# A small matrix product moved off TensorE: partial products on ScalarE and VectorE, one sum over partitions left

## The reference

```python
q = xt @ Wq.T
scores = scale * einsum('bhqd,bhkd->bhqk', qh, qh)
logits = (scores * cmask + (1.0 - cmask) * NEG) * rmask
attn = softmax(logits, axis=-1)
ctx = einsum('bhqk,bhkd->bhqd', attn, qh)
out = ctx @ Wo.T          # then x + out
```

## Time and profile before

| | |
|---|---|
| time, median of 3 runs | 1602.4 us (1602.02 to 1602.5) |
| span of the profiled execution | 1599.3 us |
| PE busy | 1513.2 us (95%) |
| PEld busy | 1185.6 us (74%) |
| DVE busy | 1198.6 us (75%) |
| ACT busy | 877.7 us (55%) |
| POOL busy | 1336.3 us (84%) |
| mean granted TensorE clock | 0.981 of full speed |

### The profile page before, as it was taken

The page is one execution under the profiler, slowest core; times in us unless marked ns, Lnnn a source line. Parts: engine busy times, 40 slices in busy tenths (PEclk is TensorE's granted clock), DMA queues, the critical chain, the costliest instruction groups (busy, mean ns, idle before and its releaser), DMA issues. The chain is left out here.

```text
span 1599.3 us, 32587 instructions
## 1 busy us (share of the span) xinstructions
PE 1513.2 (95%) x10636; PEld 1185.6 (74%) x10636; DVE 1198.6 (75%) x2676; ACT 877.7 (55%) x2189; POOL 1336.3 (84%) x1078
## 2 busy tenths in 40 slices
PE   5789999999999999999999999999999999999985
PEld 4568777777777777777777777777777777777753
DVE  4487787878778787877878787787878778787753
ACT  4345556565655656565565656556565655656441
POOL 3377989898898989889898988989898898988875
PEclk9779999999999999999999999999999999999998
DMA  4423444544444454444445444444554444454411
GB/s 137 104 65 96 108 120 109 130 123 111 118 113 117 112 130 123 110 118 115 116 113 130 123 110 119 114 117 111 130 123 111 119 113 117 111 130 96 111 53 55
DMA packets 93809, 179.07 MB, mean 112 GB/s; under 512 B 24704, under 2 KB 24832, under 8 KB 93632
## 3 DMA queue, kind: packets, MB, share of 16 engines
q1 hardware_dynamic: 64448, 109.71, 29.2%
q0 software_dynamic: 29184, 67.17, 14.9%
HBM read 36.77 MB, written 33.55 MB: 44 GB/s over the span
## 5 line engine op out<-in xcount | busy, mean ns | idle before, releaser
L835 ACT ACTIVATE small_Pt<-scores,small_kbias 108x270 f32<-108x270 f32 x1280 | 550.9, 483 | 343.7 <-PE scores L1245 334.8
L985 DVE TENSOR_REDUCE small_mxp<-max_scores 108x1 f32<-108x270 f32 x1280 | 546.7, 435 | 250.7 <-PE max_scores L1226 228.9
L646 POOL TENSOR_TENSOR small_Pacc<-small_Pacc,small_Pt 108x540 f32<-108x540 f32 x384 | 520.8, 1356 | 122.3 <-ACT small_Pt L835 116.6
L1226 PE MATMUL max_scores<-small_ops 128*108 128x270 f32 x1280 | 420.1, 336 | 22.2 <-DVE small_mxp L985 21.6
L1257 PE MATMUL ctx_psum<-small_Pt,small_V 108*64 108x270 f32 x2560 | 317.5, 395 | 0.0
L1017 DVE RECIPROCAL small_rsum<-small_rsum 128x67 f32<-128x67 f32 (+1 forms) x512 | 240.8, 532 | 66.3 <-ACT small_rsum L771 66.3
L1242 PE MATMUL scores<-small_ops 128*108 128x270 f32 x1280 | 281.1, 294 | 8.7 <-ACT small_Pt L835 7.0
L1226 PEld LDWEIGHTS max_scores<-small_ops 128*108 128x108 f32 x1280 | 221.3, 175 | 89.9 <-issue 38.4
L1257 PEld LDWEIGHTS ctx_psum<-small_Pt,small_V 108*64 108x64 f32 x2560 | 187.4, 139 | 109.0 <-issue 4.6
L1245 PE MATMUL scores<-small_ops 128*108 128x270 f32 x1280 | 265.4, 289 | 0.0
L1242 PEld LDWEIGHTS scores<-small_ops 128*108 128x108 f32 x1280 | 193.5, 174 | 38.4 <-ACT small_Pt L835 20.1
(11 more groups left out here) (129 smaller groups left out, 2273.2 us busy)
## 6 DMA issues: line engine op xcount, KB each, us to landing
small_ops<-small_H SPq DMA_DIRECT2D x512, 135.0 KB, 2.5
small_ops<-small_L SPq DMA_DIRECT2D x256, 135.0 KB, 2.5
small_ops<-small_mrow SPq DMA_DIRECT2D x128, 2.1 KB
small_xg<-x_rows,small_idx POOLq DMA_INDIRECT x80, 3.9
small_xtail<-x_rows,small_idx POOLq DMA_INDIRECT x80, 5.0
out_rows<-small_xtail,small_idx POOLq DMA_INDIRECT x80, 3.7
out_rows<-small_xg,small_idx POOLq DMA_INDIRECT x80, 4.1
wqT_sb<-wqT SPq DMA_DIRECT2D x1, 1024.0 KB, 5.4
```

Source lines behind the costliest of these rows:

```text
L646: nc.gpsimd.tensor_tensor(acc, other, t["Pt"][:R, p0], ALU.add).then_inc(pacc_step, 1)
L835: nc.scalar.activation(t["Pt"][:R, (NT * s + k) % f.NP, half, :], ST[(2 * (NT * h + k) + half) % 3][:R, 0:H], ACT.Exp, bias=t["kbias"][:R, ...
L985: nc.vector.tensor_reduce(t["mxp"][:R, h % 2, m // 2, m % 2:m % 2 + 1], MX[m % 2][:R, 0:H], AX.X, ALU.max).then_inc(mx_red, 1)
L1226: nc.tensor.matmul(MX[m % 2][:R, 0:H], ops[:, OPA, tile_cols(m // 2)], ops[:, OPB, half_cols(m % 2)], start=True, stop=True).then_inc(mx_r ...
```

## The change

The product with G is split by its four blocks. ACT multiplies block 0 by its column of xbarT into the tile `w` directly after it has copied xbarT, in step (6, 2). DVE adds blocks 1 to 3, each multiplied by its column, into `w`, in the second half of (6, 3), the second half of (6, 4) and the first half of (7, 0). The tile then holds, in each of the 128 partitions, that partition's share of the sum; PE adds the shares over the partitions with a single matmul by ones, whole in the first part of (7, 3). ACT copies that from PSUM to `w`, as before. In the last batch DVE's three stand in (6, 3) and PE's in (7, 0).

```diff
+W_SUM_AT = [(6, 3, 1), (6, 4, 1), (7, 0, 0)]
+W_AT = (7, 3)
+LAST_W_SUM_AT = [(6, 3, 0), (6, 3, 1), (6, 3, 1)]
+LAST_W_AT = (7, 0)
...
+        whole(0, "w", 0, W_AT if has_next else LAST_W_AT)
...
+        for c, at in enumerate(W_SUM_AT if has_next else LAST_W_SUM_AT):
+            table[at].append(("w_sum", c + 1))
...
                         nc.scalar.copy(t["xbarT"][:], MB[bank][:, 0:KD]).then_inc(xbar_kept, 1)
+                        if f.split:
+                            act.wait_ge(xbar_kept, b + 1)
+                            act.wait_ge(g_kept, KD)
+                            at_least(act, tail_added, f.NTAIL * b)
+                            at_least(act, out_done, NT * b)
+                            nc.scalar.mul(t["w"][:], G[:, 0, :], t["xbarT"][:, 0:1]).then_inc(w_sum_step, 1)
...
+                def w_sum(b, c):
+
+                    dve.wait_ge(w_sum_step, KD * b + c)
+                    nc.vector.scalar_tensor_tensor(out=t["w"][:], in0=G[:, c, :], scalar=t["xbarT"][:, c:c + 1],
+                                                   in1=t["w"][:], op0=ALU.mult, op1=ALU.add).then_inc(w_sum_step, 1)
...
+                    elif name == "w" and f.split:
+                        pe.wait_ge(w_sum_step, KD * (b + 1))
+                        nc.tensor.matmul(mb[:, 0:D], ones64[:, 0:1].to_broadcast([P, P]), t["w"][:],
+                                         start=True, stop=True).then_inc(w_ready, 1)
```

More of the change, by code:

```diff
@@ L44 @@
     ((4, 3), (4, 3), "proj", (4, 0)), ((4, 4), (4, 4), "proj", (4, 1)), ((5, 3), (5, 4), "proj", (5, 0)),
-    ((6, 0), (6, 1), "proj", (5, 1)), ((7, 0), (7, 1), "proj", (6, 0)), ((7, 3), (7, 4), "w", 0)]
+    ((6, 0), (6, 1), "proj", (5, 1)), ((7, 0), (7, 1), "proj", (6, 0)), ]
 V_STEPS = {1: ((0, 2, 1), (0, 3, 0)), 2: ((4, 0, 0), (4, 0, 1)), 3: ((5, 0, 0), (5, 1, 0)), 4: ((6, 3, 0), (6, 4, 0))}
@@ L48 @@
 XBAR_STEP = (6, 2, 1)
-LAST_W_AT = ((6, 4), (7, 0))
+W_SUM_AT = [(6, 3, 1), (6, 4, 1), (7, 0, 0)]
+W_AT = (7, 3)
+LAST_W_SUM_AT = [(6, 3, 0), (6, 3, 1), (6, 3, 1)]
+LAST_W_AT = (7, 0)
 LAST_W_PART_AT = [(7, 1, 1), (7, 2, 0), (7, 4, 0), (7, 4, 0), (7, 4, 1)]
@@ L128, in misc_jobs @@
         for first, last, name, arg in PAIR_STEPS:
-            if (has_prev if name == "out" else name == "w" or arg[0] < PAIRS or has_next):
-                in_chunks(name, arg, *(LAST_W_AT if name == "w" and not has_next else (first, last)))
+            if has_prev if name == "out" else arg[0] < PAIRS or has_next:
+                in_chunks(name, arg, first, last)
+        whole(0, "w", 0, W_AT if has_next else LAST_W_AT)
         if has_next:
@@ L363, in attention_kernel @@
         wlo_done = sem("wlo_done")
-        w_part_added = sem("w_part_added")
+        w_part_added, w_sum_step = sem("w_part_added"), sem("w_sum_step")
         pacc_step, tail_added = sem("pacc_step"), sem("tail_added")
@@ L1058, in alone @@
                         add_w_part(b, arg)
+                    elif name == "w_sum":
+                        w_sum(b, arg)
+                def w_sum(b, c):
+                    dve.wait_ge(w_sum_step, KD * b + c)
+                    nc.vector.scalar_tensor_tensor(out=t["w"][:], in0=G[:, c, :], scalar=t["xbarT"][:, c:c + 1],
+                                                   in1=t["w"][:], op0=ALU.mult, op1=ALU.add).then_inc(w_sum_step, 1)
                 def add_w_part(b, k):
```

## The result

| | before | after |
|---|---|---|
| time, median of 4 runs each | 1602.21 us (1601.21 to 1602.5) | 1634.09 us (1631.99 to 1635.32) |
| span of the profiled execution | 1599.3 us | 1633.3 us |
| mean granted TensorE clock | 0.981 | 0.959 |

The change makes the kernel slower: ratio 1.0198, 95% interval 1.0181 to 1.0214. Predicted were 1629 us.

The account below looks back on a forecast made before the run. PE bounds (7, 3) and (7, 4), DVE the stretch (6, 3) to (7, 2). Span 1599.3 + 24 (batches) - 1 (last batch) + 4 (clock) = 1626.3 us; median 3.1 above: 1629 us, range 1603 to 1643.

Parts of the forecast that it names:

- The likeliest case: POOL's additions block DVE's, with some falls of the clock: 1629 us, 1.7% slower, chance 0.5.
- the net loss: Loss of 3.1 us less gain of 1.5 us: 1.6 us a batch, 24 us for 15 batches.
- the clock: Behind PE's new 2.2 us wait the clock falls in a third of the batches, 0.9 us each: 4 us.
- the last batch: No max scores in these steps there; put at -1 us, between -2.9 and +1.6.
- Gain of 1.5 us in (7, 3) and (7, 4): Three of four products go from PE; DVE's chain then ends last: 1.5 us a batch, bounds 1.2 and 2.9.
- DVE's additions are held by POOL's: From (6, 3) to (7, 0), a held addition ends 0.56 us after POOL's: 1.56, 1.60 and 0.75 us.
- hardly held: Rival: DVE's three additions cost near 0.75 us each, loss 1.7 us a batch, 1605 us; chance 0.22.
- faster: Rival: PE was the bound after all, gain 2.9 us a batch with unblocked additions, 1583 us; chance 0.16.
- Loss of 3.1 us a batch: DVE's additions, 3.94 us less 0.56 idle and 0.29 from L1022, delay PE's second piece of (7, 2).
- falls in every batch: Rival: the clock costs 0.9 us in 15 batches instead of 4 us in all, 1639 us; chance 0.12.

Follow-up runs that it names:

- run 2: Changed kernel without DVE's three additions, so w holds block 0 alone; ACT's multiplication and the single product stay: 1587.27 us, ratio 0.9909.
- run 3: Changed kernel with POOL's additions of tiles 3 and 4 of head 6 left out, a one-column memset in their place: 1590.92 us, ratio 0.9928.
- run 6: Changed kernel with both DVE's three additions and POOL's two additions of head 6 left out: 1587.31 us, ratio 0.9914.
- run 11: Changed kernel with two memsets of 0.67 us in place of each of POOL's additions of tiles 3 and 4 of head 6: 1592.62 us, ratio 0.9946.
- run 1: Kernel before, four products kept on PE, with ACT's multiplication and DVE's three additions done besides and their result thrown away: 1647.47 us, ratio 1.0271.
- run 4: Changed kernel with six useless 128x512 products on PE ahead of the piece that opens (7, 0): 1620.28 us, ratio 1.0107.
- run 5: Kernel before with POOL's additions of tiles 3 and 4 of head 6 left out: 1610.06 us, ratio 1.0057.
- run 9: Changed kernel with only blocks 1 and 2 added on DVE, in (6, 4) and (7, 2), and block 3 back on PE: 1602.26 us, ratio 1.001.
- run 8: Kernel before with G and xbarT in the one-pass 32-bit format, the four products staying on PE: 1587.99 us, ratio 0.9911.
- run 7: Changed kernel with DVE's three additions moved to (6, 4), (7, 1) and (7, 2): 1704.33 us, ratio 1.0645.
- run 10: Changed kernel, DVE's additions moved to (6, 4), (7, 1) and (7, 2), POOL's token sums starting only after the third: 1613.55 us, ratio 1.0069.

## Why the prediction was right

The likeliest case came true, at 1634 us against 1629 and inside the range. The mechanism was right; that the number came so near is in part luck, since errors in both directions cancel. In the span, 1633.3 us against 1626.3, the net loss was put 7 us too high, and the clock 10, the last batch 3 and the stretch ahead of the first batch's copy 2 us too low. The time is off by 5 and not by 7 because its median lies 0.8 us above the profiled span here and not 3.1. Step by step:

- **Gain of 1.5 us in (7, 3) and (7, 4): right.** 1.55 us in the change and in runs 2, 3 and 6, with DVE's reduces as what ends last. What the prediction didn't say: with nothing lost ahead of it, half of this gain is taken back later (run 2). In the change the batch is late there, so nothing of it was.
- **DVE's additions are held by POOL's: right.** 1.46, 1.90 and 0.74 us against 1.56, 1.60 and 0.75, each held one ending 0.55 to 0.57 us after POOL. The second is longer than I had it since it starts beside POOL's addition (1401.69 and 1401.67), not 0.33 us behind its start: POOL comes 0.17 us later than I had it, since the gather ahead of it, which starts inside the first addition, takes 1.25 us and not 1.01. The rival "hardly held" falls by runs 3 and 11, and its price was wrong too: unheld additions cost 0.79 us a batch there, not 1.7, and the kernel with them is faster than the one before, where the rival had 1605 us. The rival "faster" falls by run 1 and by the 0.89 us that PE waits at (7, 1).
- **Loss of 3.1 us a batch: too high by 0.45.** The additions cost 3.97 us from start to start, 3.94 predicted, and the 0.56 us of idle time were used up. But I had left the other instructions as long as before. L1034 goes on after 0.63 us, not 1.04 (I took off 0.29 of these 0.41). And the reduces that had partly waited for PE, as the pair of 0.94 us in the earlier trace rows, find their pieces ready behind the additions and take 0.77: with the steps between them 0.33 us less. Net loss 1.1 us a batch, not 1.6.
- **The clock: the mechanism was right, the number too low.** I counted falls in a third of the batches at 0.9 us, 4 us in all. They came in 13 of 15, at some 1.1 us, 14 us by run 4. The rival "falls in every batch" had the frequency, but with the larger net loss of 1.6 us its sum is higher than what came. That the two errors, 7 us too many and 10 too few, nearly cancel is luck.
- **The last batch: wrong.** I took -1 us; from its copy of xbarT to the end it is 2.2 us longer. There the product stands in (7, 0), right behind the additions, and PE waits 2.05 us for them; the clock falls twice near there, once in the kernel before. Another 2.0 us lie ahead of the first copy of xbarT, where the change does nothing; that stretch took 152.8 to 156.2 us in the runs, whatever the kernel.

Open: why in run 1, with the same waits, the clock fell in 5 batches and not in 13; what delays ACT in run 5; and where the rest of a gain goes, beside PE's waits for POOL and the held L1105 of run 9.

## What to carry to other kernels

Work that is taken off the busiest engine must be priced at the place where it is put: look there for which engine ends last, and, for a VectorE instruction with two inputs from SBUF, for what GpSimd runs at that moment. A wait of 2 us that is new on TensorE can cost as much again by the clock (here 0.2 to 2.8 us in a batch with a fall, 1.1 in the mean), and filling it tells how much. Before work is moved at all, see whether it can be made cheaper where it is: two changed types (run 8) brought 0.9%, where three moved blocks cost 2%. The one-pass format is less exact, as the expectation of run 8 says; by how much isn't shown here.

## What the hardware showed beyond that

- An addition on VectorE is not held for one instruction of GpSimd here, but until GpSimd's row of them has a gap: 8.69 us behind six, 2.49 us with a gap behind the first (runs 7 and 10). The Trainium skill ("SBUF — State Buffer", section "Who interferes with whom") gives the shared ports to whoever issues first, for the whole instruction. In run 7 the start shown for DVE's addition lies 0.59 us ahead of the row, and it was held all the same: the order of the starts in the trace doesn't tell who is held. Whether the start shown is the moment at which the ports are taken, no run shows.
- It works the other way too: a gather's issue on GpSimd takes 1.43 us instead of 1.01 when it starts inside such a VectorE instruction (run 9).
- A new VectorE instruction that isn't held itself can still cost: in run 9 the addition takes 0.74 us, but a gather of GpSimd's beside it 0.42 us more, and the next held instruction of VectorE takes 1.66 us instead of 1.12.
